# One-hot destinations made in pairs from SBUF, in a GNN kernel's block-building loop

## The reference

```
h = max(layernorm(x), 0);  x = x + L0(h)   # mean over neighbours, two linears, layernorm
h = max(layernorm(x), 0);  x = x + L1(h)   # two graph convolutions with edge weights, row norm
h = max(layernorm(x), 0);  x = x + L2(h)   # message MLP per edge, sum per node, GRU cell, batch norm
h = max(layernorm(x), 0);  x = x + L3(h)   # weighted sum over neighbours, linear
```

## Time and profile before

| what | value |
|---|---|
| median of 3 runs | 1447.18 us (1445.31 to 1448.26) |
| profiled execution, its own time | 1448.26 us |
| its span in the trace | 1446.5 us |
| mean granted TensorE clock | 0.95 |
| busy PE / PEld / DVE / ACT / POOL | 1266.0 / 739.3 / 1021.7 / 577.6 / 712.4 us |

### The profile page before, as it was taken

How to read it: one execution, slowest core, us unless ns; L and a number is a source line. 1 busy time by engine, 2 the same in 40 slices (tenths; PEclk the granted TensorE clock), 3 DMA queues, 4 the chain that set the end, 5 groups by cost and what they waited for, 6 DMA issues and landing times.

```text
span 1446.5 us, 20064 instructions
## 1 busy us (share of the span) xinstructions
PE 1266.0 (88%) x4424; PEld 739.3 (51%) x4424; DVE 1021.7 (71%) x1900; ACT 577.6 (40%) x1462; POOL 712.4 (49%) x873
## 2 busy tenths in 40 slices
PE   4859899078898898959998989999999889997998
PEld 2534444033333333428875444544554578885775
DVE  8798253078899899850267268888898898888432
ACT  0211311066666620112011168888888723334210
POOL 0577777767787735766672166666666100000000
PEclk9989999589999998979999999999999899998999
DMA  8932512020000044443222367777776200002220
GB/s 336 335 127 67 196 53 75 23 103 19 17 26 17 10 169 167 124 155 101 87 90 98 131 208 218 232 226 222 230 223 217 57 1 0 1 0 84 73 91 35
DMA packets 87239, 167.90 MB, mean 116 GB/s; under 512 B 16108, under 2 KB 44654, under 8 KB 84628
## 3 DMA queue, kind: packets, MB, share of 16 engines
q1 hardware_dynamic: 59044, 102.19, 21.0%
q0 software_dynamic: 25472, 59.97, 13.7%
q10 hardware_dynamic: 2672, 5.11, 1.2%
HBM read 115.97 MB, written 51.25 MB: 116 GB/s over the span
## 4 chain that ended last, share of the span: by engine, by line
PE 44%; issue 17%; DVE 12%; DMA 12%; POOL 10%; DVEq 2%; POOLq 1%; ACT 0%; ACTq 0%; SPq 0%
DMA arena<-p_rows,gidx 9%; POOL cell_rows L690 9%; PE pb L1090 7%; PE pb L1206 6%; PE pb L1198 6%; PE pb L1385 5%; PE pb L1288 3%; PE pb L1356 3%; PE pb L1358 3%; PE pb L1357 3%; DVE arena L1632 2%; DMA cell_rows<-tiles,gidx 2%; PE pb L1172 2%; DVE arena L1437 1%; DVE arena L1616 1%
## 5 line engine op out<-in xcount | busy, mean ns | idle before, releaser
L801 POOL DMA_INDIRECT arena<-p_rows,gidx x184 | 189.7, 1031 | 66.9 <-issue 60.4
L736 POOL DMA_INDIRECT dst_rows<-ering,gidx x168 | 167.7, 998 | 102.5 <-issue 73.6
L690 POOL DMA_INDIRECT cell_rows<-tiles,gidx x168 | 168.3, 1002 | 67.9 <-issue 40.2
L1288 PE MATMUL pb<-arena 128*128 128x512 f32 x368 | 190.1, 599 | 5.4 <-ACT arena L961 5.4
L1632 DVE TENSOR_TENSOR arena<-pb,arena 128x384 f32 x272 | 151.8, 558 | 26.5 <-PE pb L1172 24.2
L1090 PE MATMUL pb<-ws,tiles 128*128 128x512 f32 (+1 forms) x360 | 146.5, 555 | 12.3 <-ACT tiles L823 12.3
L1741 DVE TENSOR_TENSOR arena<-pb,arena 128x512 f32<-128x512 f32 x184 | 124.3, 685 | 40.1 <-DMA arena<-p_rows,gidx 38.1
L1172 PE MATMUL pb<-arena 128*128 128x384 f32 x272 | 105.6, 515 | 45.5 <-POOL arena L743 45.4
L864 ACT ACTIVATE arena<-iota,free 128x128 f32<-128x128 f32 x272 | 94.3, 393 | 112.6 <-PE pb L1172 69.7
L1172 PE MATMUL pb<-tiles,arena 128*128 128x384 f32 x272 | 103.3, 506 | 19.7 <-DVE arena L1632 18.3
L1090 PEld LDWEIGHTS pb<-ws,tiles 128*128 128x128 f32 x360 | 67.3, 195 | 69.5 <-issue 53.5
(11 more groups left out here) (285 smaller groups left out, 2378.2 us busy)
## 6 DMA issues: line engine op xcount, KB each, us to landing
dst_rows<-arena SPq DMA_DIRECT2D x6, 2046.0 KB, 17.5
ering<-in_edge_attr_dram SPq DMA_DIRECT2D x41, 256.0 KB, 3.0
arena<-adj SPq DMA_DIRECT2D x10, 640.0 KB, 4.0
arena<-dst_rows SPq DMA_DIRECT2D x24, 264.0 KB, 2.8
arena<-wt_gru SPq DMA_DIRECT2D x48, 128.0 KB
ws<-dst_rows SPq DMA_DIRECT2D x22, 264.0 KB, 2.8
arena<-in_x_dram SPq DMA_DIRECT2D x18, 256.0 KB, 9.0
arena<-in_L_gnn_W_hh_dram SPq DMA_DIRECT2D x3, 1024.0 KB, 20.3
```

The lines of the kernel that those rows point to most:

```text
L690: nc.gpsimd.indirect_dma_start(cell_rows[:, :], bass.IndirectOffsetOnAxis(gidx[:, SPAN * a + k:SPAN * a + k + 1], 0), cring[:, a, k], None ...
L736: nc.gpsimd.indirect_dma_start(dst_rows[:, :], bass.IndirectOffsetOnAxis(gidx[:, k:k + 1], 0), ering[:, k, :], None).then_inc(e_scattered[ ...
L801: nc.gpsimd.indirect_dma_start(rows[:, k, :], None, p_rows[:, :], bass.IndirectOffsetOnAxis(gidx[:, k:k + 1], 0)).then_inc(g_landed[k], 16)
L1288: nc.tensor.matmul(e_bank(k)[:], erowT[:, k % 4], w1e_sb, start=True, stop=True).then_inc(edge_mm, 1)
```

## The change

The destination one-hots are now made for two chunks by one DVE instruction (`hots`), which reads the row 1..128 straight from `iota1` in SBUF instead of from its copy in PSUM; the copy is gone. They are made three pairs (6 chunks) ahead instead of 8 chunks ahead, ahead of the second addition of a pair, and each first waits on `block_done`. A DVE turn is 8 chunks instead of 16, so the loop has 34 turns and each loads 8 places. `dst_hot` counts pairs. On POOL, the last three of the four written-out bodies become a loop of three rounds, in which the waits compare with register values.

```
 def weights_turn(i, with_column=None):
     for q in range(TURN // 2):
-        pool.wait_ge(dst_hot, TURN * i + 2 * q + 2)
+        pool.wait_ge(dst_hot, TURN // 2 * i + q + 1)
+        passed()
...
-for i in range(EARLY):
+weights_and_edges(0)
+with pool.Fori(1, EARLY) as i:
     weights_and_edges(i)
...
-def hot(i, k):
-    vtt(ohd(k % TURN, 1)[:, :, 0], counting.unsqueeze(1),
-        cellm[:, bass.ds(2 * TURN * i + k, 1), 1:2].to_broadcast([P, 1, P]), ALU.is_equal).then_inc(dst_hot, 1)
+def hots(i, q):
+    at_least(dve, block_done, TURN * i + 2 * q - 6)
+    vtt(ohd(2 * q, 2)[:, :, 0], iota1[:].unsqueeze(1).to_broadcast([P, 2, P]),
+        cellm[:, bass.ds(TURN * i + 2 * q, 2), 1:2].to_broadcast([P, 2, P]), ALU.is_equal).then_inc(dst_hot, 1)
...
 def turn(i, last):
-    at = table_values(cell_at[0:1, bass.ds(2 * TURN * i, 2 * TURN)], (CELLS - 1) * P)
-    for k in range(2 * TURN):
-        add_block(i, k, at[k])
-        if not last or k < TURN:
-            hot(i, k + TURN)
+    at = table_values(cell_at[0:1, bass.ds(TURN * i, TURN)], (CELLS - 1) * P)
+    for q in range(TURN // 2):
+        add_block(i, 2 * q, at[2 * q])
+        if not last or q < TURN // 2 - 3:
+            hots(i + (q + 3) // 4, (q + 3) % 4)
+        add_block(i, 2 * q + 1, at[2 * q + 1])
 
-counting = pb[4][:, 0:P]
-link(nc.vector.tensor_copy(counting, iota1[:]))
...
-turns = CELL_CHUNKS // (2 * TURN)
-for k in range(TURN):
-    hot(0, k)
+turns = CELL_CHUNKS // TURN
+for q in range(3):
+    hots(0, q)
```

More of the change, by code:

```diff
@@ L1626, in add_block @@
             def add_block(i, k, at):
-                n = 2 * TURN * i + k
+                n = TURN * i + k
                 dve.wait_ge(block_done, n + 1)
```

## The result

The changed kernel takes 1458.76 us (median of 5, 1455.31 to 1464.31) where the one before takes 1447.18: slower, by a ratio of 1.009 with an interval of 1.0068 to 1.0111. The sign was right and the size was not: 11.6 us were lost, where the prediction had added up 33.

A forecast was written before the change was run, and what follows sets the result against it. DVE's chain of additions, 0.757 us apart, was taken to bound the stage. Pairs 6.9, turn's end 3.6, port 20.5 and POOL's slower loop starts 2 made 33 us on 1448.26: forecast 1481 us, range 1455 to 1500.

The forecast's parts named there:

- What bounds the stage: One-hot stage: DVE's additions, 0.757 us apart, set the pace; single one-hots fit the gap with about 0.08 us to spare.
- The pairs: Between DVE additions: a double one-hot delays the next addition to 0.809 us, 0.052 per pair, 6.9 us in all.
- The turn's end: DVE's table load and branch every 8 chunks: 1.51 us from addition to addition, 3.6 us more in all.
- the 0.3 as a bound: DVE's table load may start already 0.3 us behind the addition, the branch hiding in it: -4.6 us.
- The port: DVE one-hots reading SBUF are held while POOL multiplies: 20.5 us, plus 2 for slower starts in POOL's loop.
- held until 3.35, 0.64 us: DVE's fourth one-hot, ready at 2.71 us, waits for POOL's third multiplication; 0.64 us in each of 32 turns.
- The rest: One-hots made 6 chunks ahead instead of 8, POOL's loop register work, the dropped PSUM copy: nothing added.
- DVE is not held: Rival: in the stage only POOL is held by DVE, never DVE by POOL; 1459 to 1466 us, chance 0.20.
- The clock: Rival: with PE idle more, part of the stage runs at granted clock 0.50; 1494 to 1527 us, chance 0.10.
- Not slower: Rival: double one-hots fit the gap, DVE and POOL never meet, the load hides; 1443 to 1448 us, chance 0.08.
- To the end: Behind the stage: a microsecond won or lost in the stage reaches the kernel's end once.

The follow-up runs named there:

- e1: The changed kernel with the double one-hot's row 1..128 read from its copy in PSUM again; 1449.90 us, ratio 1.0021 to the kernel before.
- e2: The kernel before with the row 1..128 of its single one-hots read from SBUF instead of PSUM; 1493.48 us, ratio 1.0328.
- e4: The changed kernel with POOL's four bodies written out again instead of one and a loop of three; 1455.23 us, ratio 1.0058 to the kernel before.
- e9: The changed kernel with POOL's indirect DMA behind the fourth multiplication of a turn instead of the second; 1470.68 us, ratio 1.0162 to the kernel before.
- e6: The changed kernel with POOL's indirect DMA behind the first multiplication of a turn instead of the second; 1460.62 us, ratio 1.0097 to the kernel before.
- e8: The changed kernel with DVE turns of 16 chunks again, pairs and SBUF input kept; 1461.98 us, ratio 1.0101 to the kernel before.
- e10: The kernel before with the places loaded two at a time instead of 16 at a turn's start; 1469.63 us, ratio 1.0142.
- e11: The kernel before with the places loaded four at a time instead of 16 at a turn's start; 1440.53 us, ratio 0.9941.

## Why the prediction was right or wrong

- **What bounds the stage.** Right. The chain of additions, 0.75 us each, sets it in every kernel here, and the one-hots are free while they fit the gap.
- **The pairs.** 6.9 us forecast. e1 has 0.75 and 0.80 us in turn, 0.04 over the old pace for a pair: 133 x 0.04 = 5.3 us. Right.
- **The turn's end.** This step failed, by 10 us: it said 1.51 us per end, 3.6 us more in all. Measured are 1.18, and 1.23 in e1, 0.43 to 0.47 over the pace per 8 chunks, where half of the old end is 0.66: some 6 to 7 us less in all. The load took 0.595 instead of 0.68 us and started 0.3 us behind the addition instead of 0.55. The text had the 0.3 as a bound, priced at -4.6 us, but kept the one-hot's delay in its own value. Pairs and end together came out at e1's 0.9 us, not 10.5.
- **The port.** The mechanism was right, both ways (e2), and it is the cause of the loss (e1). Its term was mis-sized: 20.5 + 2 us against 12.6 (245.5 - 232.9), of which e4 puts 3.7 on POOL's loop. So the step "held until 3.35, 0.64 us", times 32, failed: the hold measured 0.27 us. It took each one-hot to come 1.15 us behind the last. Between the third and the fourth one-hot of a POOL turn lies DVE's turn's end, since one-hots are made three pairs ahead, and the text had set the end behind the fourth. In the text's own terms, counted from the second one-hot's end (402.79), the fourth starts at 3.17 and not 2.71, and the third multiplication, later in POOL's loop, ends at 3.56 and not 3.35; the one-hot is let go some 0.12 us before that recorded end (an estimate, worked out in the last section). 3.56 - 0.12 - 3.17 = 0.27. What the text left out is smaller: the holds behind the two copies (some 3 us in sum). The sum of all the stretches, 14.5 us, is more than the 12.6 because a turn's end here is 1.18 us and in e1 1.23. e9, which moves the two apart, lengthens a turn by 0.39 us and the stage by 7.5; e6 shows them hiding each other the other way round. e8 agrees.
- **The rest.** The shorter lead and the new wait on `block_done` cost nothing that e1 shows: 0.9 us in all.
- **The rivals.** "DVE is not held" gave 1459 to 1466, nearest to the measured 1458.76, for the wrong reason: e2 excludes it, and multiplications stayed at 1.04 us. The range of 1455 to 1500 holds the measured time only because it had been stretched down into that rival's case. The clock kept 1.00. "Not slower" had the load's early start right and missed that holds happen.
- **To the end.** The stage grew by 13.5 us and the median by 11.6. In the profiled execution only 4.4 us are left at the end: it is 13.1 us late behind the stage, 7.0 at the first addition of the gather stage (836.9 before, 843.9 after) and 4.4 at the end, though the change touches none of these stages. At 1453.09 us it was also faster than all five runs behind the median; totals of e1 (0.9 us of stage, 1442.4 us of span) scatter likewise. Why single executions differ there was not looked into.

## What to carry to other kernels

Where DVE works beside POOL instructions that read SBUF, keep one of its two inputs in PSUM: the place of one small constant was worth 13 us in one arrangement and 47 in another, with no change in an undisturbed instruction's length. Before adding up two stalls per turn, draw one turn on both engines: stalls that are neighbours are paid once. And sequencer work (table loads, branches) belongs behind the instruction whose end is waited for anyway, in pieces short enough for that wait.

## What the runs showed that I had not expected

- The length of a table load isn't even in its count: 0.306 us for one place, 0.52 for two (e10), 0.35 for four (e11), 0.595 for eight, 1.10 for sixteen. Why two take longer than four was not tried.
- A held DVE instruction starts in the record at its usual time and is stretched; the waits show nothing of it. In the changed kernel and e9 it ended 0.29 to 0.30 us behind the recorded end of POOL's multiplication though it needs 0.41, so by my estimate it was let go some 0.12 us before that end.
- While a DVE instruction is held, its sequencer goes on: a table load behind it and behind one more queued addition starts meanwhile and costs nothing (e6, 0.74 us for a turn's end).
